# First four expert tiles at fixed places, tile 0's weights split during routing, tile 1's weights ordered by tile 0's rows

## The reference

```python
xn = _modulate(_ln(x), sh_mlp, sc_mlp)
xf = xn.reshape(-1, C)
gate_logits = xf @ w_gate
topk_logits, topk_idx = jax.lax.top_k(gate_logits, TOP_K)
gates = jax.nn.softmax(topk_logits, axis=-1)
cw = jnp.sum(jax.nn.one_hot(topk_idx, NUM_EXPERTS, dtype=xf.dtype) * gates[..., None], axis=1)
hmid = jax.nn.gelu(jnp.einsum('tc,ech->eth', xf, w1) + b1[:, None, :], approximate=True)
eo = jnp.einsum('eth,ehc->etc', hmid, w2) + b2[:, None, :]
moe = jnp.einsum('te,etc->tc', cw, eo).reshape(B, N, C)
```

## Time and profile before

| | |
|---|---|
| median of 3 runs | 1709.09 us (1708.98 to 1716.18) |
| the profiled execution, its own time | 1716.46 us |
| its span, first to last instruction | 1714.7 us |
| mean granted TensorE clock | 0.957 of full |
| busy share: PE, DVE, ACT, POOL | 90%, 74%, 57%, 45% |

### The profile page before, as it was taken

One profiled execution on the slowest core, in us unless ns is written; L12 is line 12 of the kernel. 1 busy time (PEld: TensorE's weight loads), 2 busy tenths in 40 slices (PEclk: granted clock), 3 DMA queues, 4 the chain that ended last, 5 costly groups with the idle time before them and its releaser, 6 DMA issues.

```text
span 1714.7 us, 29220 instructions
## 1 busy us (share of the span) xinstructions
PE 1537.8 (90%) x9121; PEld 990.8 (58%) x9121; DVE 1267.8 (74%) x2311; ACT 980.0 (57%) x1726; POOL 764.0 (45%) x1655
## 2 busy tenths in 40 slices
PE   6889999856899999996789999899898999989998
PEld 4732223645799988885532223688774222358885
DVE  7788886763898686667688887767888888765653
ACT  4647776433566555553457777543654777763432
POOL 0556630252565644205666666666766666200000
PEclk9999999968899999998799999999999999999999
DMA  6564334055645654315443334211046233400001
GB/s 167 141 170 89 73 80 95 15 53 160 166 134 146 146 165 130 102 53 159 122 111 87 84 73 99 43 5 19 4 101 172 68 88 69 113 1 1 1 1 56
DMA packets 112185, 152.60 MB, mean 89 GB/s; under 512 B 36661, under 2 KB 91943, under 8 KB 111932
## 3 DMA queue, kind: packets, MB, share of 16 engines
q1 hardware_dynamic: 105340, 135.64, 27.0%
q0 software_dynamic: 6720, 15.44, 9.0%
HBM read 113.99 MB, written 32.62 MB: 86 GB/s over the span
## 4 chain that ended last, share of the span: by engine, by line
PE 60%; DVE 18%; issue 7%; DMA 6%; SPq 4%; ACT 3%; POOL 1%; DVEq 0%; ACTq 0%; POOLq 0%
PE psum L1385 18%; PE psum L1530 8%; PE psum L1519 8%; PE psum L1682 7%; PE psum L1505 7%; PE psum L1813 4%; DVE minus_max L2134 3%; DMA k_stack<-qk_parts_d 2%; DVE bn L2042 1%; PE psum L1442 1%; DVE x_norm L2064 1%; SPq L764 1%; PE psum L1569 1%; SPq L804 1%; DVE hid_lo L2525 1%
## 5 line engine op out<-in xcount | busy, mean ns | idle before, releaser
L2134 DVE TENSOR_REDUCE minus_max<-psum 128x2 bf16<-128x1024 f32 x384 | 452.7, 1219 | 80.6 <-PE psum L1505 73.9
L1285 ACT ACTIVATE probs<-psum 128x512 f32<-128x512 f32 x768 | 418.5, 600 | 153.5 <-PE psum L1519 151.3
L1385 PE MATMUL psum<-x_split,w_hi 128*128 128x512 f32 x684 | 257.9, 418 | 12.4 <-DVE x_tail L2081 5.6
L1519 PE MATMUL psum<-q_stack,k_stack 109*128 109x512 bf16 x768 | 261.1, 387 | 7.3 <-ACT probs L1285 5.3
L1505 PE MATMUL psum<-k_stack,q_stack 108*128 108x512 bf16 x720 | 220.9, 389 | 14.5 <-DVE minus_max L2134 9.7
L906 POOL TENSOR_TENSOR qr_m<-qr_m 64x8 f32<-64x8 f32 (+35 forms) x544 | 197.3, 363 | 42.6
L1519 PEld LDWEIGHTS psum<-q_stack,k_stack 109*128 109x128 bf16 x768 | 72.7, 98 | 244.1 <-ACT probs L1285 179.3
L1530 PE MATMUL psum<-probs,v_stage 128*32 128x512 f32 x1536 | 203.9, 604 | 1.1 <-ACT o_t L1274 1.1
L1385 PEld LDWEIGHTS psum<-x_split,w_hi 128*128 128x128 f32 x684 | 132.8, 194 | 41.0 <-issue 9.0
L901 POOL TENSOR_TENSOR qr_m<-qr_rows 64x288 f32<-64x288 f32 (+31 forms) x64 | 46.3, 724 | 240.7 <-DMA qr_rows<-qr_rows 240.7
L1385 PE MATMUL psum<-x_split,w_lo 128*128 128x512 f32 x342 | 138.3, 404 | 0.0
(11 more groups left out here) (364 smaller groups left out, 3321.9 us busy)
## 6 DMA issues: line engine op xcount, KB each, us to landing
qk_parts_d<-qk_parts SPq DMA_DIRECT2D x36, 384.0 KB, 4.9
raw_b<-in_L_cond_w SPq DMA_DIRECT2D x30, 432.0 KB, 4.1
raw_a<-in_L_cond_w SPq DMA_DIRECT2D x30, 384.0 KB
q_stack<-qk_parts_d SPq DMA_DIRECT2D x48, 216.0 KB
k_stack<-qk_parts_d SPq DMA_DIRECT2D x48, 216.0 KB
q_stack<-qk_parts_d SPq DMA_DIRECT2D x48, 144.0 KB
k_stack<-qk_parts_d SPq DMA_DIRECT2D x48, 144.0 KB
moe_out_d<-branch SPq DMA_DIRECT2D x11, 576.0 KB, 3.1
```

Of the source, the lines that this page charges most:

```text
L1285: act.activation(PE_[:, v // 4, v % 4, :], psum[:, score_bank(v), :], ACT.Exp, scale=SCALE).then_inc(s_e, 1)
L1385: i = pe.matmul(dst, a, r, start=(n == 0), stop=(n == len(terms) - 1))
L1519: pe.matmul(psum[:, score_bank(v), :], K6[0:STK + 1, g % 4, h, P * kt:P * kt + P], Q6[0:STK + 1, g % 4, h, :], start=True, stop=True).then ...
L2134: dve.tensor_reduce(MX[:, g % 2, 2 * u:2 * u + 2], psum[:, o:o + 2, :], AX.X, ALU.max, negate=True).then_inc(s_mx, 1)
```

## The change

It has six parts.

1. `tile_table` marks the first tile of every expert as present (before: of expert 0 alone), whether it has tokens or not. So tiles 0 to 3 always begin at slots 0, 2048, 4096 and 6144 and have experts 0 to 3, and `tile_rows` and `tile_expert` give constants for them.
2. The token numbers `TID` move to other memory, and the wait for all scatters ahead of the first `tile_parts` goes.
3. The six splits of tile 0's weights on VectorE move from behind `tile_table` (w1) and behind tile 0's turned rows (w2) into the routing.
4. In `moe_loads` tile 1's b2, w1 and w2 are issued once tile 0's rows have landed (`m_x[0]`), before the waits for the table and the scatters. The token list of tile 1 comes after them.
5. SP then waits until tile 1's rows have landed (`m_x[1]`) before it issues the L3 loads.
6. `turn_at(0)` is 6 instead of 5.

```diff
-        TID = at("token_numbers", [P, NT], I32, rb + 51200)
+        TID = at("token_numbers", [P, NT], I32, top[0] - NT * 4)
...
         def turn_at(t):
-            return 5 if t == 0 else 2
+            return 6 if t == 0 else 2
...
-                r = 0 if t == 0 else sp.value_load(TBL[0:1, t:t + 1], min_val=0, max_val=MOE_ROWS - N)
+                r = t * TOK if t < EXPERTS else sp.value_load(TBL[0:1, t:t + 1], min_val=0, max_val=MOE_ROWS - N)
...
-                return bass.ds(sp.value_load(TBL[0:1, 12 + t:13 + t], min_val=0, max_val=EXPERTS - 1), 1)
+                return bass.ds(t if t < EXPERTS else sp.value_load(TBL[0:1, 12 + t:13 + t], min_val=0, max_val=EXPERTS - 1), 1)
...
-                sp.wait_ge(s_tb, 1)
+                sp.wait_ge(m_x[0], 16 * TT)
                 e = tile_expert(1)
-                sp.wait_ge(s_sd, 32 * 16)
-                load_tokens(1)
                 load_tile_b2(1, e)
                 for i in range(3):
                     load_tile_w1(1, i, e)
+                for i in range(3):
                     load_tile_w2(1, i, e)
+                sp.wait_ge(s_tb, 1)
+                sp.wait_ge(s_sd, 32 * 16)
+                load_tokens(1)
+                sp.wait_ge(m_x[1], 16 * TT)
                 sp.wait_ge(s_scd, 48)
...
-                link(dve.memset(M16[:, 0, 0:1], 1.0))
+                link(dve.memset(M16[:, 0, :], 1.0))
...
-                if j == 0:
-                    dve.wait_ge(s_sd, 32 * 16)
                 dve.wait_ge(m_hh, j + 1)
...
                 slot_hits(0)
+                split_lo_first(0, "1", 0)
+                split_lo_first(0, "1", 1)
                 logit_rows(2)
                 gate_ranks(2)
+                split_lo_first(0, "1", 2)
                 slots(2)
                 slot_hits(1)
+                for i in range(3):
+                    split_lo_first(0, "2", i)
                 logit_rows(3)
...
                 tile_table()
-                for i in range(3):
-                    split_lo_first(0, "1", i)
                 tile_tails(0)
                 for c in range(KC + 1):
                     tile_low(0, c)
-                for i in range(3):
-                    split_lo_first(0, "2", i)
```

## The result

| | before | after |
|---|---|---|
| median, 8 runs each, same chip | 1712.53 us (1708.98 to 1716.3) | 1722.53 us (1714.96 to 1726.44) |
| ratio of after to before | | 1.0045, 95% interval 1.0027 to 1.0063 |
| the profiled execution | 1716.46 us, span 1714.7 | 1724.69 us, span 1722.9 |

The change made the kernel slower, by 0.45% or about 7.7 us (4.6 to 10.8 us by the interval; the medians are 10.0 us apart). Forecast were +1.4 us and a range of 1702 to 1717 us. The class, within 0.5% either way, holds by the ratio itself, but its interval reaches past 0.5%.

The account below looks back on a forecast made before the run. TensorE was taken to stand until the L3 loads land, which sets the tile stream. Landing 0.5 us sooner and the turn 1.9 us later gave +1.4 us, 1709.1 + 1.4 = 1710.5 us; range 1702 to 1717.

Parts of the forecast that it names:

- w1 splits: VectorE in routing: three splits of 2.7 and 1.9 us fit into idle time before batch 2's logits and slots; 0.
- w2 splits: VectorE between batch 1's hits and batch 3's logits, no idle time there: everything behind up to 3.0 us later; 3.0 taken.
- list issued to first gather: Tile 1's token list on SP to its first gather's start: 1.9 us, as in the earlier trace.
- gathers and their landing: Tile 1's four gathers: last issued 3.9 us after the first, landing in 4.0 us (2.9 to 8.4).
- issue to landing: L3 loads starting on an empty queue: 13.8 us, the middle of 10.4 and 17.2; landing at 430.8, 0.5 us sooner.
- landing to tile 2's first turn: TensorE after the L3 landing: 0.4 us for one more chunk turned, 1.5 us before tile 1's first unit; 1.9 us later.
- The step that failed: SP's queue: tile 1's weights issued by about 402, through by 405, before the token list; held against the slower rival.
- The term for the scatters: Batch 3's scatters beside tile 1's weights: cost 0 to 4.4 us, 2.2 taken, so counted at 406.8.
- The right rival: Weights hold up scatters and gathers, L3 loads starting at 424, landing at 438; slower by over 0.5%, up to 1720.5; chance 0.11.
- the second rival: L3 loads at the best rate, 369 GB/s, landing at 427: 1706.7 us, or 1704 with w2 splits hidden; chance 0.17.
- unit 0: TensorE at tile 0's start: the scatter wait and its 5.26 us stall go, worth 0 while L3 loads land after 418.
- Signs named beforehand: Among them: no unit 0 stall, logits about 3 us later, one 13 to 17 us stall, L3 issued at 415 to 419.

Follow-up runs that it names:

- the weights issued early: Changed kernel without SP's waits for tile 0's and tile 1's rows, so tile 1's weights go out once their buffers are free: ratio to before 0.9965.
- the early stall removed: Changed kernel with SP's loads in the order of the kernel before, without the wait for tile 1's rows, the rest as changed: ratio to before 1.0006.

## Why the prediction was wrong

**What bounds the kernel: right.** The landing of the L3 loads sets the stream, as three kernels show from three sides: the weights issued early (tiles begin 11 us later, kernel faster), the skew entries moved (no stall, kernel faster), the early stall removed (nothing gained).

**Step by step, on before's scale:**

| step | forecast | after |
|---|---|---|
| w1 splits | 0 | 0, they lie in idle gaps |
| w2 splits | +3.0 | +2.1 at batch 3's logits, +1.5 at the last scatter |
| tile 0's rows | 390.2 | 390.5 |
| token list issued | 407.1 | 407.9 |
| list issued to first gather | 1.9 us | 8.8 us |
| gathers and their landing | 3.9 + 4.0 us | 3.8 + 2.7 us |
| L3 loads issued | 417.0 | 423.2 |
| issue to landing | 13.8 us | 14.6 us |
| landing | 430.8 | 437.8 |
| landing to tile 2's first turn | +1.9 | +1.0 |
| sum | +1.4 | +7.5 |

The sum of after is 6.5 us (437.8 against 431.3) and 1.0; the measured ratio makes it 7.7 us.

**The step that failed** is the sentence "SP has issued the weights by about 402, and they should be through by 405, before the token list", and with it the 1.9 us from the list's issue to the first gather. SP issued the last weight at 407.8 on before's scale, in 17.5 us, and the queues still moved 372 GB/s two microseconds before the list had landed (418 to 420 us of its own time). So the list landed behind them, 6.9 us later than in the earlier trace rows. The 1.9 us was the landing of a list that has the queues to itself, and the sum moved the list behind 3024 KB of weights without asking what that does to its landing. With batch 3's scatters left out the same step took 4.9 us behind the same weights, so of the 6.9 us about 3 are the weights alone and 4 the scatters' hold on them. The issue times of the weights had been taken from a stretch in which no scatter was in flight.

**The term for the scatters was too small as well, hidden by others.** It was 2.2 us with an upper bound of 4.4, from the gathers. Measured, the last scatter's count came 5.3 us later without the row wait, 4.8 us in after with the skew entries at unit 9 and 6.7 us with the list on GpSimd. In after itself only a bound shows: the last scatter was issued at 398.67 and counted by 413.35, 14.7 us or less, at most 4.8 us over 9.87. Two things covered the miss. The last scatter was issued 1.5 us later than before's and not 3.0, and SP was late itself, so that the wait for the scatters was through at once when SP came to it, at 407.9. That the place in the sum came out 0.8 us from the forecast was luck. The bounds were taken from gathers; scatters beside weights took longer.

**The right rival had 0.11.** "The weights hold up the scatters and gathers" is what happened, with one direction missing: it was mainly the scatters that held up the weights, and through them the list. It named the L3 loads' start at 424 us as the point from which it decides. They start at 423.2, and land at 437.8 where it needed 438. What the prediction held against it was the failed step itself. The rule of the Trainium skill beside it ("DMA: Bandwidth & Descriptors", section "Queues, rings and completion order") also has each DMA engine finish a whole packet of one queue before it turns to another; that fits weights that stand while many small writes go, but no run here shows what happens inside a packet, and the counts (89 packets of weights against 32 of the scatters in 8 us) don't look like taking turns one by one. When 96 packets of the scatters moved, in 404 to 408 us, the weights moved at 228 GB/s beside them.

**The range.** It ended at 1717. On the median of 1709.1 that the forecast stood on, 7.7 us more is 1716.8. Over eight runs the median of before was 1712.5, and 3.4 us of the miss of 12.0 are that; 7.7 - 1.4 = 6.3 us are the failed step; the rest is how medians and the ratio differ. The upper bound of the rival, 1720.5, had been worked out and cut off; it lies under the measured median too. That the class came out right, with 0.81 on it, is luck: the sum was off by 6 us and the threshold lay at 8.5.

**Turn, unit 0, L3 time: right.** The gap of 1.45 us stands at 456.10 where 1.5 was forecast; unit 0 has no stall; 13.8 us for the L3 loads were 14.6. The turn's price was 2.1 us by the two kernels run side by side, yet the table has +1.0: with the turn back at 5 the same stretch is 0.8 us shorter than in before, and what gives that back isn't known.

**Signs named beforehand.** No stall at unit 0, batch 3's logits later and the gap of 1.5 us came true, the scatters counted before 412 too. The L3 loads issued at 415 to 419 (423.2) and the stall of 13 to 17 us (23.5) did not.

**One reading was wrong.** The prediction takes 369 GB/s for the best 2 us of before's trace. In the whole trace 744 to 746 us moved 418. It changes nothing above: at 418 GB/s the second rival's loads would be under 1 us shorter, and they measured 14.6 us.

## What to carry to other kernels

Before a large transfer is moved ahead of a small one on which a chain hangs, price the small one's landing behind it, not its landing alone; and before it is moved beside scatters of single elements, expect both to be slow until the scatters are counted. When one load releases a stall, look first at who needs it and whether that need can wait: here one number that moved the skew entries by five units gave 0.9946 (0.9919 with the next list ahead of the large loads), where the best reordering of transfers alone gave 0.9965; the intervals of 0.9946 and 0.9965 overlap. A dependency on a semaphore that nothing needs (the L3 loads behind tile 1's rows) puts every delay of its chain on the path.

## What was not expected of the hardware

- Scatters of 128 single numbers each are slow to count: the last of eight is counted 9.87 us after its issue with 0 GB/s moving, and 14.6 to 16.5 us after it in the chains with the weights issued right at tile 0's rows.
- While they are in flight other transfers can nearly stop: 13 GB/s over 8.1 us in after, then 249 and 207 GB/s, then 58 to 85 until 416 us; and 256 in 4 us with the scatters left out.
- SP's issues are held up in such a stretch: 4.15 us and 3.48 us for single ones, 7.95 us for three, for 1.39 us for three with no scatters. In after, issues cost their usual time where over 200 GB/s moved (404 to 408 us).
- A transfer of 2 KB lands in 8.57 us behind weights in the same queue, and in 14.61 us behind the L3 loads (before with the skew entries at unit 9); in before its landing and the start of the first gather together took 1.9 us.
